# A graph layer's second block per pair as three f32r products, with the powers, the shift and the vector engine's order rearranged

## The chip, the cores and the metric

The kernel runs on one core of a Trainium2 chip. Its time is the device time of one execution in microseconds (us). The core has five engines that run their own instruction streams and meet at semaphores: TensorE (PE; its weight loads are listed as PEld), VectorE (DVE), ScalarE (ACT), GpSimd (POOL) and SyncE (SP), which here only issues DMAs.

## The reference

```python
h = concatenate([x[row], x[col]], axis=-1)          # 25,000 edges, 50,000 nodes, D = 256
msgs = silu(h @ W1.T + b1) @ W2.T + b2
agg = segment_sum(msgs, row) / (cnt + 1e-08)
gi, gh = agg @ w_ih.T + b_ih, x @ w_hh.T + b_hh
r, z = sigmoid(i_r + h_r), sigmoid(i_z + h_z)
n = tanh(i_n + r * h_n)
x_new = (1.0 - z) * n + z * x
gnn = gamma * (x_new - mean) / sqrt(var + 1e-05) + beta
out = layernorm(x + gnn)
```

## The kernel before, in words

There are two stages. The edge stage (0 to about 940 us of the span) makes a message of 768 numbers per edge, already multiplied with `w_ih`, and stores it to DRAM as a high and a low f32r part. The node stage (from about 948 us) takes the 50,000 nodes as 392 blocks of 128, two blocks (h = 0 and 1) to a pair, 196 pairs. One pair is one turn of every engine. `node_turns` writes the order of each engine by hand: a list of (part, lag), where in the step for pair q the engine does `part` for pair q + lag. The first 12 steps are written out, the middle is a loop whose body holds four steps (QU = 4, the number of buffers of most tiles), the last ones are written out again. Every wait is on a semaphore counter `S[...]` that its producer raises once a pair.

For one pair: POOL gathers the messages of both blocks (`gather_rows`, tile `mg`, an indirect DMA each, after `copy_rows` has put four row numbers into `rows_now` for every second pair). DVE makes one-hot matrices (`one_hot`, tile `oh`), PE adds the messages to nodes (`segment_sum`, eight f32r products), ACT scales the sums by the counts (`mean_scale`), PE adds x times `whh` in fp32 and the bias (`node_products`, lines mm L938), ACT takes the sigmoids (`gates`, tile `rz`). Then DVE: `gated_h` (rhn), `n_input` (npre); ACT: `tanh` (nt); DVE: `subtract_n` (diff), `z_diff` (zd), `x_new` (xn), `stats1` (st), `aggregate1` (ag), every second turn `var_eps1` (ve from ag); POOL: `inv_std1` (a power -0.5 of the four variances of two pairs, tile rs1, L420) and `add_beta` (xb = x + beta, L413); DVE: `scale_gamma` (tg), `residual` (uu, with its sum by accumulator), `minus_mean` (nm); ACT: `squares` (with accumulator); DVE: `var_eps2` (ve from sq); POOL: `inv_std2` (two variances, tile rs2, L428); DVE: `shift` (nmr); ACT: `last_norm` (yy); SP stores yy.

DVE's order in a step, and POOL's:

```python
node_turns(dve, ((gated_h, -1), (n_input, -1), (var_eps2, -5), (residual, -4), (one_hot, 2), (minus_mean, -4),
                 (subtract_n, -1), (z_diff, -1), (x_new, -1), (scale_gamma, -3), (stats1, -1), (shift, -5),
                 (aggregate1, -1), (var_eps1, -1)), first=-2, last=5)
node_turns(pool, ((gather_rows, 4), (inv_std1, -2), (inv_std2, -5), (add_beta, -2)), first=-4, last=5)
node_turns(pe, ((products0, 0), (segment_sum, 1), (products1, 0)), first=-1, last=0)
```

`segment_sum` of pair q + 1 waits for `n_input` of pair q - 1, since two sets of PSUM banks alternate.

Of the kernel before, what the change touches and what calls it, by code (L numbers as in the profile page):

```python
# [63 lines left out]
def gnn_layer(nc, x, xt, src, dst, w1t, b1, w2, b2, wiht, whht, bih, bhh, gamma, beta, consts, out):  # L64
# [4 lines left out]
    with ctx:  # L69
# [6 lines left out]
        def sems(name, n):  # L76
# [19 lines left out]
        whh = sb("whh", [P, KC, G3])  # L96
        bias_hn = sb("bias_hn", [P, D], f32r)
# [50 lines left out]
        tg = sb("tg", [P, 2, 2 * D])  # L148
        st1, ag1 = sb("st1", [P, QU, 2, 6]), sb("ag1", [P, QU, 2, 2])
# [11 lines left out]
        idx_ready, w1_hi, w1_ready = sem("idx_ready"), sem("w1_hi"), sem("w1_ready")  # L161
        b2_ready, wc_mm, wc_hi, wc_lo = sem("b2_ready"), sem("wc_mm"), sem("wc_hi"), sem("wc_lo")
# [22 lines left out]
                 " n_s1 n_a1 n_v1 n_r1 n_tg n_u n_nm2 n_sq2 n_v2 n_r2 n_nmr n_y").split()  # L185
# [77 lines left out]
        def _(sp):  # L263
# [63 lines left out]
            def load_x(q, u):  # L327
                need(sp, S["n_mm"], q - QU + 1)
                sp.dma_start(xts[:, u, :], xt[bass.ds(q * P, P), :]).then_inc(got_xt[u], 16)
# [12 lines left out]
            node_turns(sp, ((store_y, -7), (load_counts, 3), (load_x, 3), (load_rows, 2)), first=-3, last=7)  # L342
# [10 lines left out]
        def _(pool):  # L353
# [35 lines left out]
            def node_stage(summed):  # L389
                def copy_rows(q, u):  # L390
                    need(pool, S["n_oh"], q - QU + 2)
                    nc.gpsimd.tensor_copy(rows_now[:, 2 * u:2 * u + 4], slot_row[:, bass.ds(2 * q, 4)])\
                        .then_inc(idx_now, 1)
                    pool.wait_ge(idx_now, 2 * E_TURNS + duo(q, u))

                def gather_rows(q, u):
                    if u % 2 == 0 and not summed:
                        copy_rows(q, u)
                    for h in range(2):
# [5 lines left out]
                        else:  # L405
                            gather(to, rows_now[:, 2 * u + h:2 * u + h + 1], messages, got_m[2 * u + h], last_row)

# [44 lines left out]
        def _(act):  # L452
# [681 lines left out]
```

## Time and profile before

| | |
|---|---|
| median of three runs | 2369.15 us (2367.12 to 2369.52) |
| the profiled execution's own time | 2368.18 us |
| its span, first to last instruction | 2366.2 us |
| busy over the span: PE, DVE, ACT, POOL | 96%, 84%, 63%, 61% |
| mean granted TensorE clock | 0.991 of full |
| 1000 to 2300 us | 184 turns of 7.07 us |

A busy share says how long an engine had an instruction in it, not that it set the pace. PE's is over all matmuls, which overlap each other, so it is read by the distance from one start to the next. For DVE too, instructions overlap a little: the next one can start before the last one's end, and the distance of starts is what an instruction costs.

### The profile page before, as it was taken

To read this page: it belongs to the slowest core of one execution; us is meant where nothing else is said; L and a number is where in the kernel's file an instruction comes from. 1 tells how busy PE (TensorE), PEld (TensorE's weight loads), DVE (VectorE), ACT (ScalarE), POOL (GpSimd) and SP (SyncE) were. 2 spreads that over 40 slices of the span, in tenths; PEclk is the share of its full clock that TensorE was granted. 3 is DMA by queue.
4 is the path that set the end of the run, shared out by engine and by line. 5 is a ranking of instruction groups with operands and counts; after the bars stand their busy time and mean duration, and the time that the engine had idled before them with its cause. 6 is when DMAs were issued, how large, how long until landed. Compare 5 with 4: busy or idle time off the path is not lost.

```text
span 2366.2 us, 46571 instructions
## 1 busy us (share of the span) xinstructions
PE 2278.3 (96%) x10226; PEld 1620.5 (68%) x10226; DVE 1993.6 (84%) x6129; ACT 1500.4 (63%) x2959; POOL 1437.9 (61%) x1479
## 2 busy tenths in 40 slices
PE   6999999999999998899999999999999999999995
PEld 4888888888888886566666666666666666666663
DVE  6777777777777776599999999999999999999998
ACT  3444444444444444477777777777777777777776
POOL 5444444444444441577777777777777777777774
PEclk9999999999999999899999999999999999999998
DMA  4666666666666665666766666666666666666663
GB/s 150 232 231 230 230 231 231 231 228 230 230 229 228 230 232 201 209 222 227 227 227 226 224 229 223 225 222 222 215 223 225 225 223 220 227 219 225 224 217 112
DMA packets 192885, 521.09 MB, mean 220 GB/s; under 512 B 51393, under 2 KB 53977, under 8 KB 192857
## 3 DMA queue, kind: packets, MB, share of 16 engines
q1 hardware_dynamic: 116752, 313.91, 37.1%
q0 software_dynamic: 75264, 206.47, 27.1%
q10 hardware_dynamic: 840, 0.40, 0.1%
q8 instruction: 9, 0.15, 0.0%
q14 instruction: 20, 0.16, 0.0%
HBM read 468.80 MB, written 206.73 MB: 285 GB/s over the span
## 4 chain that ended last, share of the span: by engine, by line
PE 39%; DVE 24%; POOL 16%; issue 16%; DVEq 2%; POOLq 1%; DMA 1%; ACT 0%; SPq 0%; ACTq 0%
PE banks L938 35%; POOL rs L420 6%; POOL mg L347 5%; PE banks L950 4%; DVE zd L869 3%; DVE xn L875 3%; DVE st L916 3%; POOL rs L428 3%; DVE rhn L852 3%; DVE diff L864 3%; DVE tg L880 2%; POOL xb L413 2%; DVE uu L891 2%; DVE ag L922 2%; DVE oh L843 2%
## 5 line engine op out<-in xcount | busy, mean ns | idle before, releaser
L938 PE MATMUL banks<-whh,xts 128*128 128x512 f32 (+1 forms) x3136 | 1089.5, 485 | 0.0
L938 PEld LDWEIGHTS banks<-whh,xts 128*128 128x128 f32 x3136 | 552.2, 190 | 312.5 <-issue 281.8
L347 POOL DMA_INDIRECT mg<-messages,rows_now x392 | 467.9, 1194 | 171.2 <-issue 80.3
L347 POOL DMA_INDIRECT xsrc<-in_x,src_now x196 | 187.1, 954 | 419.3 <-PE banks L950 412.0
L413 POOL TENSOR_TENSOR xb<-xs,betab 128x512 f32<-128x512 f32 x196 | 250.6, 1279 | 198.5 <-DVE ag L922 198.5
L938 PE MATMUL banks<-mg,oh 128*128 128x512 f32 (+1 forms) x1568 | 323.6, 348 | 35.6 <-DVE npre L858 17.6
L480 ACT ACTIVATE msg<-banks 128x512 fp32r<-128x512 f32 (+1 forms) x392 | 192.6, 491 | 244.3 <-PE banks L938 217.1
L542 ACT ACTIVATE banks<-banks,rcount 128x768 f32<-128x768 f32 x392 | 326.7, 871 | 32.2 <-PE banks L938 22.5
L938 PEld LDWEIGHTS banks<-mg,oh 128*128 128x128 f32 x1568 | 253.8, 189 | 126.8 <-issue 75.0
L645 DVE TENSOR_TENSOR msg<-banks,msg 128x512 fp32r<-128x512 f32 (+1 forms) x392 | 200.0, 552 | 152.2 <-ACT msg L480 152.2
L554 ACT ACTIVATE yy<-uu,nmr,rs 128x256 f32<-128x256 f32 x392 | 214.0, 593 | 169.1 <-DVE nmr L911 169.1
L938 PE MATMUL banks<-bias_hn,ones 128*128 128x256 f32 x392 | 266.9, 681 | 0.0
L938 PE MATMUL banks<-wsh,silh 128*128 128x512 f32 (+1 forms) x784 | 264.1, 337 | 2.8 <-DVE msg L645 2.8
L938 PE MATMUL banks<-wsl,silh 128*128 128x512 f32 (+1 forms) x784 | 263.8, 337 | 0.0
L938 PE MATMUL banks<-wsh,sill 128*128 128x512 f32 (+1 forms) x784 | 263.2, 336 | 0.0
L530 ACT ACTIVATE rz<-banks 128x512 f32<-128x512 f32 x392 | 229.0, 584 | 4.8 <-PE banks L938 4.8
L347 POOL DMA_INDIRECT xdst<-in_x,dst_now x196 | 186.5, 951 | 65.1 <-issue 64.8
L548 ACT ACTIVATE nt<-npre 128x512 f32<-128x512 f32 x196 | 123.9, 632 | 155.3 <-DVE npre L858 155.3
L461 ACT ACTIVATE eh<-banks 128x512 fp32r<-128x512 f32 x196 | 117.4, 599 | 164.7 <-PE banks L950 154.5
L564 ACT ACTIVATE yy<-uu,nm 128x256 f32<-128x256 f32 x392 | 194.7, 503 | 2.5 <-DVE nm L900 2.5
L891 DVE SCALAR_TENSOR_TENSOR uu<-tg,rs,xb 128x256 f32<-128x256 f32 x392 | 173.7, 481 | 0.0
L880 DVE SCALAR_TENSOR_TENSOR tg<-xn,ag,gammab 128x256 f32<-128x256 f32 x392 | 171.2, 478 | 0.0
(128 smaller groups left out, 4151.6 us busy)
## 6 DMA issues: line engine op xcount, KB each, us to landing
messages<-msg SPq DMA_DIRECT2D x196, 772.0 KB, 3.3
xts<-in_xt SPq DMA_DIRECT2D x196, 256.0 KB, 6.7
xs<-in_x SPq DMA_DIRECT2D x196, 256.0 KB, 3.6
out_y<-yy SPq DMA_DIRECT2D x196, 256.0 KB, 3.5
mg<-messages,rows_now POOLq DMA_INDIRECT x392, 7.5
xsrc<-in_x,src_now POOLq DMA_INDIRECT x196, 3.5
xdst<-in_x,dst_now POOLq DMA_INDIRECT x196, 2.9
oh<-counts SPq DMA_DIRECT2D x196, 2.0 KB
```

What stands on the lines that cost most here:

```text
L347: nc.gpsimd.indirect_dma_start(out=dst_tile, out_offset=None, in_=rows, in_offset=bass.IndirectOffsetOnAxis(ap=table, axis=0), bounds_chec ...
L413: nc.gpsimd.tensor_tensor(out=xb[:, u, :], in0=xs[:, u, :], in1=betab[:, :], op=ALU.add)\
L420: nc.gpsimd.tensor_tensor(out=rs1[:, u - 1:u + 1, :].rearrange("p q h -> p (q h)"), in0=ve1[:, u - 1:u + 1, :].rearrange("p q h -> p (q h) ...
L480: nc.scalar.activation(msg[:, u % EU, n0:n1], p_g[:, part, 0:n1 - n0], ACT.Copy).then_inc(e_gh[part], 1)
L530: nc.scalar.activation(rz[:, u % 2, h, :], pn[u % 2][:, h, 0, :], ACT.Sigmoid).then_inc(S[f"n_rz{h}"], 1)
L542: nc.scalar.activation(sums_now, sums_now, ACT.Copy, scale=rcount[:, bass.ds(q * 2 + h, 1)])\
L554: last = nc.scalar.activation(yy[:, u, h * D:(h + 1) * D], uu[:, u, h * D:(h + 1) * D], ACT.Identity, bias=nmr[:, u, h:h + 1], scale=rs2[: ...
L564: last = nc.scalar.activation(yy[:, u, h * D:(h + 1) * D], uu[:, u, h * D:(h + 1) * D], ACT.Square, bias=nm2[:, u, h:h + 1], accum_out=sq2 ...
L645: nc.vector.tensor_tensor(msg[:, u % EU, HALF + n0:HALF + n1], p_g[:, part, 0:n1 - n0], msg[:, u % EU, n0:n1].bitcast(f32), ALU.subtract). ...
L880: last = nc.vector.scalar_tensor_tensor(out=tg[:, u % 2, h * D:(h + 1) * D], in0=xn[:, u, h * D:(h + 1) * D], scalar=ag1[:, u, h, 0:1], in ...
L891: last = nc.vector.scalar_tensor_tensor(out=uu[:, u, h * D:(h + 1) * D], in0=tg[:, u % 2, h * D:(h + 1) * D], scalar=rs1[:, u, h:h + 1], i ...
L938: return nc.tensor.matmul(out_, lhsT, rhs, start=start, stop=stop, skip_group_check=skip)
```

## The change

The second block of each pair (h = 1) no longer multiplies x in fp32: ACT copies the block's x to f32r (`x_hi`, tile xh), POOL subtracts that from x (`x_lo`, tile xl), and PE does three f32r products (high by high, high by low, low by high) with f32r halves of the weights, which are made once in the edge stage by an ACT copy and a DVE subtraction, while ACT waits for the latter. `inv_std2` takes the powers of two pairs at once, `shift` and `last_norm` come later (lag -7 for -5 and -6), `squares` writes its unused main output into xn and no longer into yy, `copy_rows` goes ahead by a step, and the orders of POOL, ACT and DVE change.

```diff
+        wxh, wxl = sb("wxh", [P, KC, G3], f32r), sb("wxl", [P, KC, G3], f32r)
+        xh, xl = sb("xh", [P, QU, D], f32r), sb("xl", [P, QU, D], f32r)
...
             def load_x(q, u):
+                need(sp, S["n_xl"], q - QU + 1)
                 need(sp, S["n_mm"], q - QU + 1)
...
-            node_turns(sp, ((store_y, -7), (load_counts, 3), (load_x, 3), (load_rows, 2)), first=-3, last=7)
+            node_turns(sp, ((store_y, -8), (load_counts, 3), (load_x, 3), (load_rows, 2)), first=-4, last=8)
...
+                def x_lo(q, u):
+                    if not isinstance(q, int) or q >= 5:
+                        pool.wait_ge(S["n_tg"], q - 3)
+                    pool.wait_ge(S["n_xh"], q + 1)
+                    need(pool, S["n_mm"], q - QU + 1)
+                    nc.gpsimd.tensor_tensor(out=xl[:, u, :], in0=xts[:, u, D:2 * D], in1=xh[:, u, :].bitcast(f32),
+                                            op=ALU.subtract).then_inc(S["n_xl"], 1)
...
                 def inv_std2(q, u):
-                    pool.wait_ge(S["n_v2"], q + 1)
-                    need(pool, S["n_y"], q - QU + 1)
-                    nc.gpsimd.tensor_tensor(out=rs2[:, u, :], in0=ve2[:, u, :], in1=halves[:, 0:2], op=ALU.pow)\
-                        .then_inc(S["n_r2"], 1)
-
-                node_turns(pool, ((gather_rows, 4), (inv_std1, -2), (inv_std2, -5), (add_beta, -2)), first=-4, last=5)
+                    if u % 2 == 1:
+                        pool.wait_ge(S["n_v2"], q + 1)
+                        need(pool, S["n_y"], q - QU + 1)
+                        nc.gpsimd.tensor_tensor(
+                            out=rs2[:, u - 1:u + 1, :].rearrange("p q h -> p (q h)"),
+                            in0=ve2[:, u - 1:u + 1, :].rearrange("p q h -> p (q h)"),
+                            in1=halves[:, :], op=ALU.pow).then_inc(S["n_r2"], 1)
+
+                node_turns(pool, ((inv_std1, -2), (inv_std2, -5), (x_lo, 1), (add_beta, -2), (gather_rows, 4), (copy_rows, 5)), first=-5, last=5)
...
+            nc.scalar.activation(wxh[:, :, :], whh[:, :, :], ACT.Copy).then_inc(wx_hi, 1)
+            act.wait_ge(wx_lo, 1)
             act.wait_ge(rb_mm, 1)
...
+            def x_hi(q, u):
+                act.wait_ge(got_xt[u], 16 * (nth(q, u) + 1))
+                need(act, S["n_mm"], q - QU + 1)
+                nc.scalar.activation(xh[:, u, :], xts[:, u, D:2 * D], ACT.Copy).then_inc(S["n_xh"], 1)
...
-            node_turns(act, ((last_norm, -6), (tanh, -1), (gates0, 0), (mean_scale, 1), (squares, -4), (gates1, 0)), first=-1, last=7)
+            node_turns(act, ((tanh, -1), (gates0, 0), (mean_scale, 1), (x_hi, 2), (gates1, 0), (last_norm, -7), (squares, -4)), first=-2, last=7)
...
+            dve.wait_ge(wx_hi, 1)
+            nc.vector.tensor_tensor(wxl[:, :, :], whh[:, :, :], wxh[:, :, :].bitcast(f32), ALU.subtract).then_inc(wx_lo, 1)
...
             def x_new(q, u):
                 dve.wait_ge(S["n_zd"], q + 1)
+                need(dve, S["n_sq2"], q - QU + 1)
...
             def shift(q, u):
-                dve.wait_ge(S["n_r2"], q + 1)
+                dve.wait_ge(S["n_r2"], duo(q, u))
...
-            node_turns(dve, ((gated_h, -1), (n_input, -1), (var_eps2, -5), (residual, -4), (one_hot, 2), (minus_mean, -4),
-                             (subtract_n, -1), (z_diff, -1), (x_new, -1), (scale_gamma, -3), (stats1, -1), (shift, -5),
-                             (aggregate1, -1), (var_eps1, -1)), first=-2, last=5)
+            node_turns(dve, ((gated_h, -1), (n_input, -1), (shift, -7), (var_eps2, -5), (var_eps1, -2), (residual, -4), (minus_mean, -4),
+                             (subtract_n, -1), (z_diff, -1), (x_new, -1), (one_hot, 2), (scale_gamma, -3), (stats1, -1),
+                             (aggregate1, -1)), first=-2, last=7)
...
+                        if h == 0:
+                            last = mm(to, xts[:, u, c * P:(c + 1) * P], whh[:, c, n0:n1], False, c == KC - 1, True)
+                        else:
+                            hi, lo = (t[:, u, c * P:(c + 1) * P] for t in (xh, xl))
+                            mm(to, hi, wxh[:, c, n0:n1], False, False, True)
+                            mm(to, hi, wxl[:, c, n0:n1], False, False, True)
+                            last = mm(to, lo, wxh[:, c, n0:n1], False, c == KC - 1, True)
```

## Rows read from the trace of the kernel before

**Rows 1.** Loop, 1000 to 2300 us: busy PE, PEld, DVE, ACT, POOL; clock, DMA

```profile
1000.00:2300.00 1300.00, 1280.73 (x4786) 812.22 (x4785) 1230.80 (x3772) 987.40 (x2026) 970.73 (x920) 1.00 0.68 223
```

**Rows 2.** Waits, same stretch: total us, times, longest

```profile
DVE nmr L911 <- POOL rs L428: 17.3, 90, 1.1
PE banks L938 <- DVE npre L858: 17.2, 47, 1.0
DVE rhn L852 <- issue: 15.7, 44, 0.4
```

**Rows 3.** Timeline of DVE: start us, us busy, what, [idle before]

```profile
1679.50 0.25 DVE L922 BATCH_NORM_AGGREGATE ag<-st 128x2 f32<-128x6 f32 x2
1679.67 0.69 DVE L852 TENSOR_TENSOR rhn<-rz,banks 128x512 f32<-128x512 f32 x1
...
1680.99 0.16 DVE L905 TENSOR_SCALAR ve<-sq 128x2 f32<-128x2 f32 x1
...
1685.31 0.74 DVE L916 BATCH_NORM_STATS2 st<-xn 128x6 f32<-128x256 f32 x2
1685.97 0.14 DVE L911 TENSOR_TENSOR nmr<-nm,rs 128x2 f32<-128x2 f32 x1
1686.20 0.25 DVE L922 BATCH_NORM_AGGREGATE ag<-st 128x2 f32<-128x6 f32 x2
1686.60 0.69 DVE L852 TENSOR_TENSOR rhn<-rz,banks 128x512 f32<-128x512 f32 x1
...
1692.24 0.75 DVE L916 BATCH_NORM_STATS2 st<-xn 128x6 f32<-128x256 f32 x2
...
1693.29 0.25 DVE L922 BATCH_NORM_AGGREGATE ag<-st 128x2 f32<-128x6 f32 x2
1693.89 0.69 DVE L852 TENSOR_TENSOR rhn<-rz,banks 128x512 f32<-128x512 f32 x1 [0.36 <-issue]
...
1700.58 0.25 DVE L922 BATCH_NORM_AGGREGATE ag<-st 128x2 f32<-128x6 f32 x2
...
1701.07 0.69 DVE L852 TENSOR_TENSOR rhn<-rz,banks 128x512 f32<-128x512 f32 x1
```

**Rows 4.** Timeline of DVE near the end of the kernel

```profile
2352.02 0.08 DVE L891 DVE_READ_ACCUMULATOR uu<-tg,rs,xb 128x1 f32 x1
2352.13 0.17 DVE L900 TENSOR_SCALAR nm<-usum 128x2 f32<-128x2 f32 x1
2352.21 0.87 DVE L880 SCALAR_TENSOR_TENSOR tg<-xn,ag,gammab 128x256 f32<-128x256 f32 x2
2353.00 1.22 DVE L911 TENSOR_TENSOR nmr<-nm,rs 128x2 f32<-128x2 f32 x1
```

**Rows 5.** Timeline of POOL near the end of the kernel

```profile
2352.87 1.33 POOL L413 TENSOR_TENSOR xb<-xs,betab 128x512 f32<-128x512 f32 x1
```

**Rows 6.** Timeline of POOL in the loop

```profile
1686.67 1.28 POOL L413 TENSOR_TENSOR xb<-xs,betab 128x512 f32<-128x512 f32 x1 [1.08 <-DVE ag L922]
1688.10 1.31 POOL L347 DMA_INDIRECT mg<-messages,rows_now  x1 [0.15 <-issue]
...
1690.97 1.47 POOL L420 TENSOR_TENSOR rs<-ve,halves 128x4 f32<-128x4 f32 x1
```

**Rows 7.** Timeline of PE in the loop

```profile
1681.22 1.64 PE L938 MATMUL banks<-mg,oh 128*128 128x512 f32 x8
1682.69 1.88 PE L938 MATMUL banks<-whh,xts 128*128 128x512 f32 x4
1684.01 0.68 PE L938 MATMUL banks<-bias_hn,ones 128*128 128x256 f32 x1
...
1686.70 0.68 PE L938 MATMUL banks<-bias_hn,ones 128*128 128x256 f32 x1
```

**Rows 8.** The gathers into mg in the loop, from issue to landing

```profile
DMA to landing us min/median/max: 4.8/7.5/9.2
```

**Rows 9.** Timeline of ACT at the weights' preparation

```profile
34.81 0.60 ACT L499 ACTIVATE bias_c<-banks 128x512 f32<-128x512 f32 x1 [1.71 <-PE banks L938]
```

**Rows 10.** Waits of DVE, 965 to 1003 us, the first turns

```profile
DVE rhn L852 <- PE banks L938: 6.1, 4, 2.8
```

More of the change, by code:

```diff
@@ L161, in gnn_layer @@
         idx_ready, w1_hi, w1_ready = sem("idx_ready"), sem("w1_hi"), sem("w1_ready")
+        wx_hi, wx_lo = sem("wx_hi"), sem("wx_lo")
         b2_ready, wc_mm, wc_hi, wc_lo = sem("b2_ready"), sem("wc_mm"), sem("wc_hi"), sem("wc_lo")
@@ L184, in gnn_layer @@
         names = ("n_oh n_sg0 n_sg1 n_sc0 n_sc1 n_g0 n_g1 n_mm n_rz0 n_rz1 n_rhn n_npre n_tanh n_diff n_xb n_zd n_xn"
-                 " n_s1 n_a1 n_v1 n_r1 n_tg n_u n_nm2 n_sq2 n_v2 n_r2 n_nmr n_y").split()
+                 " n_xh n_xl n_s1 n_a1 n_v1 n_r1 n_tg n_u n_nm2 n_sq2 n_v2 n_r2 n_nmr n_y").split()
         S = {n: sem(n) for n in names}
@@ L390, in copy_rows @@
                 def copy_rows(q, u):
[L391 to L394, printed above, removed]
+                    if u % 2 == 0 and not summed:
+                        need(pool, S["n_oh"], q - QU + 2)
+                        nc.gpsimd.tensor_copy(rows_now[:, 2 * u:2 * u + 4], slot_row[:, bass.ds(2 * q, 4)])\
+                            .then_inc(idx_now, 1)
                 def gather_rows(q, u):
                     if u % 2 == 0 and not summed:
-                        copy_rows(q, u)
+                        pool.wait_ge(idx_now, 2 * E_TURNS + duo(q, u))
                     for h in range(2):
@@ L560, in squares @@
                 need(act, S["n_v2"], q - QU + 1)
-                need(act, n_stored[u], 16 * nth(q, u))
                 for h in range(2):
-                    last = nc.scalar.activation(yy[:, u, h * D:(h + 1) * D], uu[:, u, h * D:(h + 1) * D], ACT.Square,
+                    last = nc.scalar.activation(xn[:, u, h * D:(h + 1) * D], uu[:, u, h * D:(h + 1) * D], ACT.Square,
                                                 bias=nm2[:, u, h:h + 1], accum_out=sq2[:, u, h:h + 1])
@@ L903, in var_eps2 @@
                 dve.wait_ge(S["n_sq2"], q + 1)
-                need(dve, S["n_r2"], q - QU + 1)
                 nc.vector.tensor_scalar(ve2[:, u, :], sq2[:, u, :], 1.0 / D, EPS_LN, ALU.mult, ALU.add)\
@@ L1079, in node_products, with with_x @@
             def node_products(q, u, h):
-                pe.wait_ge(got_xt[u], 16 * (nth(q, u) + 1))
+                if h == 0:
+                    pe.wait_ge(got_xt[u], 16 * (nth(q, u) + 1))
+                else:
+                    pe.wait_ge(S["n_xl"], q + 1)
                 pe.wait_ge(S[f"n_sc{h}"], q + 1)
                 o = pn[u % 2]
-                for c in range(KC):
-                    last = mm(o[:, h, 0, :], xts[:, u, (2 * h + c) * P:(2 * h + c + 1) * P], whh[:, c, 0:2 * D],
-                              False, c == KC - 1, True)
-                last.then_inc(S[f"n_g{h}"], 1)
+                def with_x(to, n0, n1):
+                    for c in range(KC):
+                        if h == 0:
+                            last = mm(to, xts[:, u, c * P:(c + 1) * P], whh[:, c, n0:n1], False, c == KC - 1, True)
+                        else:
+                            hi, lo = (t[:, u, c * P:(c + 1) * P] for t in (xh, xl))
+                            mm(to, hi, wxh[:, c, n0:n1], False, False, True)
+                            mm(to, hi, wxl[:, c, n0:n1], False, False, True)
+                            last = mm(to, lo, wxh[:, c, n0:n1], False, c == KC - 1, True)
+                    return last
+                with_x(o[:, h, 0, :], 0, 2 * D).then_inc(S[f"n_g{h}"], 1)
                 mm(o[:, h, 1, D:2 * D], ones[:, :], bias_hn[:, :], False, False, True)
-                for c in range(KC):
-                    last = mm(o[:, h, 1, D:2 * D], xts[:, u, (2 * h + c) * P:(2 * h + c + 1) * P], whh[:, c, 2 * D:G3],
-                              False, c == KC - 1, True)
-                return last
+                return with_x(o[:, h, 1, D:2 * D], 2 * D, G3)
             def products0(q, u):
```

## The prediction

> **What bounds the kernel now.** The page first suggests TensorE, which is busy for 96% of the span. I then asked for the node stage alone, since almost the whole change lies there: in 1300 us of its loop PE is busy for 1280.7 us and DVE for 1230.8 [rows 1]; 184 turns fit, so a turn is 7.07 us. Two engines near their full time call for a third view, the waits. PE waits for DVE's npre 47 times, about once in every four turns (17.2 us in all), and no wait of DVE for PE is in the list; DVE's own waits are for POOL's power rs before nmr (17.3 us) and an "issue" idle time of 0.36 us once per body of the loop, at its branch [rows 2]. So DVE leads and PE follows. The PE timeline agrees: the sums' eight f32r products take from 1681.22 to 1682.69, 1.47 us, and a fp32 half 2.69 us from one bias product to the next (1684.01 to 1686.70) [rows 7], so PE needs 1.47 + 2 x 2.69 = 6.85 us a turn and has some 0.2 us left. DVE needs 7.07 less what it waits. In the first turns, where DVE lacks the later parts, it is the other way round: DVE waits for PE four times [rows 10].
>
> The question is then what the change does to the distances between DVE's starts. I read those from one turn to the next.
>
> **The change part by part, DVE first; all per turn.**
>
> *The wait for rs2 goes.* From the first st to the first ag it is 0.89 us in the turn without the wait (1685.31 to 1686.20) and 1.05 in the next (1692.24 to 1693.29) [rows 3]. The longer form comes in half the turns, 90 waits in 184 [rows 2]. Hence 0.16 / 2: -0.08. In the new order shift takes a power made two turns earlier, so this should go entirely; at worst (POOL still late) nothing is gained.
>
> *var_eps1 moves* from behind ag, which it waits for, to the middle of small instructions. Before, ag to rhn is 0.17 us without it (1679.50 to 1679.67) and 0.40 and 0.49 with it (1686.20 to 1686.60, 1700.58 to 1701.07) [rows 3]. So 0.23 or 0.32 more in half the turns, 0.14 a turn. In its new place a small instruction costs its issue slot, 0.07 to 0.08 (nm to what follows it, 2352.13 to 2352.21 [rows 4]; its own 0.17 mostly overlaps the next), in half the turns 0.04. Net -0.10; bounds -0.14 and -0.07.
>
> *nmr moves* out of a place where it was free: ag waits for st anyway, and 0.23 us lie between nmr and ag (1685.97 to 1686.20) [rows 3]. Without nmr that gap stays, as ag follows st's end. Behind npre nmr costs its slot: +0.07, at most its own 0.16.
>
> *minus_mean loses its cover.* one_hot stood between uu and nm and moves behind xn. At the end of the kernel, where no one_hot is left, the order uu, nm is already there: nm starts 0.11 us after the accumulator read (2352.02 to 2352.13) [rows 4], whereas in the loop one_hot starts with that read. one_hot costs the same in either place. +0.11; the lower bound is nothing, the upper one 0.2, if diff's own wait for a landing comes late behind nm as well.
>
> *nmr and xb collide.* At the end of the kernel nmr, an operation on two columns that takes 0.14 in the loop [rows 3], takes 1.22 us, from 2353.00 to 2354.22 [rows 4], and POOL's xb runs from 2352.87 to 2354.20 [rows 5]. It was held up until xb was nearly done. In the loop the first candidate today is ve, 1.32 us behind rhn (1679.67 to 1680.99) [rows 3], and xb starts behind ag and takes 1.28 [rows 6], so it is just over in time. In the new order rhn is never held back by ve, while xb still waits for ag: it starts some 0.07 (1686.67 against 1686.60) to 0.2 us behind rhn, later in relation to it by what ve1 used to take. nmr at 1.32 then can wait between nothing and 0.13 us. I take +0.05, the middle rounded down, because ve is never held in the loop today. The Trainium skill, in SBUF — State Buffer, section Who interferes with whom, says that a DVE instruction with two SBUF inputs and a GpSimd instruction that reads SBUF exclude each other, and that whichever is issued first blocks the other. Rows 4 and 5 agree; by its rule every lateness of xb past that point goes to DVE in full, which speaks against taking ve1 out ahead of rhn.
>
> Sum for DVE: -0.08 - 0.10 + 0.07 + 0.11 + 0.05 = +0.05 us a turn. x_new's extra wait (squares a turn earlier) and gated_h's waits stay covered, see ACT and PE.
>
> *PE.* The second half takes twelve f32r products for eight fp32 instructions. Eight f32r ones of the same two widths take 1.47 [rows 7], so twelve 2.2, with the bias product's 0.1 about 2.3 for 2.69: 0.4 us less. PE falls to some 6.45 and just waits longer for npre: nothing on the path. If this cover were gone, x_lo or x_hi late, PE has 0.6 us to absorb it. Only the first turns gain: three of the four waits there (the first one, 2.8 us, is the filling) [rows 10] shrink by 0.4: -1.2 us once.
>
> *ACT* is busy for 987 / 184 = 5.4 us a turn [rows 1]; the copy of 256 columns adds about 0.4 to 0.6. 5.9 of 7.1: hidden. x_hi stands in front of gates1, whose result DVE wants at rhn, over 1.5 us later. tanh now comes first, and DVE wants it at diff: the path npre, nmr, ve, uu, nm to diff is about 1.7 us by the distances above, and tanh of 512 columns needs 0.6 to 0.7. squares comes last in ACT's step and ends before the next tanh; its queue holds nothing that DVE waits for before x_new.
>
> *POOL.* xb to the first gather 1.43, two gathers 2.87 to the power, the power 1.46 [rows 6], half a copy 0.1, and x_lo. x_lo has half of xb's columns: 0.64 if all of xb's 1.28 scales, 1.28 if nothing does; as fixed parts of POOL instructions are small (the copy of four columns) I take 0.73. Together 6.6, and up to 0.2 for the sequencer: 6.6 to 6.8 of 7.1. The second power of each second pair vanishes (it is now one of four columns every second turn, in the turn without inv_std1). So POOL keeps the pace, with 0.3 to 0.5 us to spare. x_lo waits for tg, and add_beta and the gathers are queued behind it; as add_beta waits for the later ag anyway, that wait costs nothing. The gathers come a turn later than before: the second starts some 3 us into a turn and its one_hot reads it 4.9 us into the next one, so it has 8.9 to 9 us, against 7.5 in the median and 9.2 at most [rows 8]. A few turns may wait 0.1: under 1 us in all. With one_hot in its old place, 2.2 us into the turn, it would have had 6.3 and lost.
>
> *SP.* load_x waits for x_lo too, which is a turn older; load_rows still waits for xb at the turn's end and is the last of its step. xts is wanted a turn earlier, by x_hi; it is issued three pairs ahead. Nothing.
>
> *Once.* In the edge stage ACT copies 1536 columns: 0.60 us for 512 [rows 9], so at most 1.8, and 1.5 with a fixed part of 0.15. Then it waits for DVE's subtraction, by the 0.69 us of a 512-column one and the columns' share about 1.8. Before, ACT waited 1.71 us there [rows 9]; 3.3 - 1.7 = +1.6 us, and PE waits behind bias_c. At the end the last power has four columns instead of two and comes in the same chain: +0.5.
>
> **Total.** 184 turns x 0.05 = 9.2. The 12 turns before the loop's start have no wait for rs2, so the other four terms hold, +0.13 for the eight that DVE paces: 1.0. Then -1.2 + 1.6 + 0.5. Sum +11.1 us on the profiled execution's 2368.2: 2379.3. The median of the runs is 1 us above that execution, so 2380.
>
> **The rivals.**
> - *A wait behind its producer is free* (faster). If nm behind uu costs nothing, the turn is 0.05 - 0.11 = -0.06: -11 + 1 = -10, so 2359. For it: only one place of the trace has this order. Against it: that place shows 0.11, and DVE's chain is otherwise gapless. It decides from a cost of nm, nmr and the collision together under 0.17 us. The Trainium skill, in VectorE: DVE Perf Modes, section The DRAIN you can't avoid, says that a semaphore between DVE instructions costs nothing extra. By that rule this rival would be the case; the 0.11 in rows 4 is against it. 0.23, taken with the milder forms in which nmr's slot is free too (2346).
> - *TensorE paces part of the turns after all* (faster). If the 0.36 us at rhn once in four turns were PE and not the branch, 0.09 a turn would go: 0.05 - 0.09 = -0.04, 2362. For it PE's 98% in rows 1; against it the row's "issue" and PE's waits for DVE. 0.07.
> - *The terms cancel* within 0.2%: 0.15.
> - *POOL becomes late* (slower by more). If x_lo takes 1.28 or a gather is late, POOL needs 7.2 to 7.4 us, xb comes late, and DVE's nmr is held by as much: +0.2 a turn, 39 us and more, 2410 to 2430. For it: the spare time is only 0.3 to 0.5 us. 0.14.
> - *My forecast*, slower by 0.2 to 1.3%: 0.41.
>
> **How the numbers follow.** A measurement of this kernel can tell about 0.2% (5 us) from no change. Faster 0.30 (the first two), same 0.15, slower 0.55. The likeliest case's own range is 2374 to 2400; the bounds of its terms added up give -0.08 - 0.14 + 0.07 + 0 + 0 = -0.15 and, the wait gone, -0.08 - 0.07 + 0.16 + 0.2 + 0.13 = +0.34, or 2341 to 2437. For 8 in 10 I leave out the outermost parts: 2348 to 2412.
>
> **What would show it right or wrong.** In the new trace: no wait of DVE nmr for POOL; nm 0.11 behind the accumulator read; nmr near 0.15 to 0.2 us long and not 1 us; PE waiting for npre in every turn, by 0.5 us and more; DVE's busy share of the loop up, from 94.7%; x_lo near 0.73, within st. Wrong would be: nm following at once, a turn under 7.0, DVE waiting for PE, mg or POOL, or nmr long.

## The result: 2421 us, 2.2% slower, and the profile after

The changed kernel takes 2421.18 us (median of 4 runs, 2419.53 to 2421.72), the kernel before beside it 2369.28. The ratio is 1.022, with a 95% interval of 1.0202 to 1.0238. The profiled execution's span is 2419.3 us, before it was 2366.2. I had forecast 2380 with a range up to 2412: the direction is right, the size is not. Of the runs further down, one execution each of d3 and d4 took over twice the time of the others and is left out of their medians.

First the loop's busy time from 1000 to 2300 us (PE, PEld, DVE, ACT, POOL, then clock and DMA), to be held against [rows 1]:

```profile
1000.00:2300.00 1300.00, 1164.26 (x5336) 840.62 (x5335) 1221.31 (x3646) 1002.10 (x2130) 1026.72 (x978) 1.00 0.66 216
```

PE is busy for 116 us less, and everything takes longer all the same: fewer turns fit, and DVE starts 3646 instructions for 3772. DVE's busy share is 93.9% for 94.7%; it fell, where the forecast's list of signs had it rise, since the added time lies between instructions. The waits of the same stretch (total us, times, longest) against [rows 2]:

```profile
PE banks L964 <- DVE npre L883: 135.7, 178, 2.2
POOL xl L419 <- DVE tg L906: 124.0, 175, 1.8
POOL xb L427 <- DVE ag L948: 60.7, 175, 0.5
DVE ag L948 <- DVE st L942: 27.1, 178, 0.2
DVE rhn L877 <- issue: 17.7, 42, 0.4
DVE oh L868 <- DMA mg<-messages,rows_now: 2.6, 6, 0.8
```

PE waits for npre in every turn now, 0.76 us each time; POOL waits for DVE twice a turn; DVE's wait of nmr for the power is gone. What is left to DVE is waiting for itself (ag behind st), the loop's branch and six waits for a gather. So DVE sets the turn. The DVE timeline over one turn and the top of the next, shortened (start, busy time, what it does, idle time before), against [rows 3, 4]:

```profile
1711.70 0.69 DVE L877 TENSOR_TENSOR rhn<-rz,banks 128x512 f32<-128x512 f32 x1
1712.42 0.69 DVE L883 TENSOR_TENSOR npre<-rhn,banks 128x512 f32<-128x512 f32 x1
1713.02 0.15 DVE L937 TENSOR_TENSOR nmr<-nm,rs 128x2 f32<-128x2 f32 x1
1713.09 0.16 DVE L931 TENSOR_SCALAR ve<-sq 128x2 f32<-128x2 f32 x1
...
1713.97 0.08 DVE L917 DVE_READ_ACCUMULATOR uu<-tg,rs,xb 128x1 f32 x1
1714.09 0.45 DVE L926 TENSOR_SCALAR nm<-usum 128x2 f32<-128x2 f32 x1
1714.17 0.69 DVE L889 TENSOR_TENSOR diff<-xs,nt 128x512 f32<-128x512 f32 x1
1714.89 0.71 DVE L894 TENSOR_TENSOR zd<-rz,diff 128x512 f32<-128x512 f32 x1
...
1717.58 0.74 DVE L942 BATCH_NORM_STATS2 st<-xn 128x6 f32<-128x256 f32 x2
1718.47 0.25 DVE L948 BATCH_NORM_AGGREGATE ag<-st 128x2 f32<-128x6 f32 x2 [0.15 <-DVE st L942]
1718.64 0.69 DVE L877 TENSOR_TENSOR rhn<-rz,banks 128x512 f32<-128x512 f32 x1
1719.36 0.69 DVE L883 TENSOR_TENSOR npre<-rhn,banks 128x512 f32<-128x512 f32 x1
1719.96 0.33 DVE L937 TENSOR_TENSOR nmr<-nm,rs 128x2 f32<-128x2 f32 x1
1720.22 0.15 DVE L931 TENSOR_SCALAR ve<-sq 128x2 f32<-128x2 f32 x1
```

And POOL beside it:

```profile
1711.86 1.27 POOL L427 TENSOR_TENSOR xb<-xs,betab 128x512 f32<-128x512 f32 x1 [0.20 <-DVE ag L948]
...
1714.88 1.00 POOL L352 DMA_INDIRECT mg<-messages,rows_now  x1 [0.30 <-issue]
...
1717.74 0.73 POOL L419 TENSOR_TENSOR xl<-xts,xh 128x256 fp32r<-128x256 f32 x1 [0.22 <-DVE tg L906]
1719.01 1.27 POOL L427 TENSOR_TENSOR xb<-xs,betab 128x512 f32<-128x512 f32 x1 [0.55 <-DVE ag L948]
```

The reader is to see three things. nm starts 0.12 us behind the accumulator read (1713.97 to 1714.09). ag starts 0.89 us behind the first st (1717.58 to 1718.47) in every turn. And nmr is 0.15 us long in one turn and 0.33 in the next: in the first xb starts 0.16 us behind rhn (1711.70 to 1711.86), in the second 0.37 (1718.64 to 1719.01), ends at 1720.28, and ve starts at 1720.22.

A single turn misleads, since the loop's body holds four turns that differ. I therefore worked out from the timelines of both kernels the mean distance from each DVE start to the next, over the node turns 12 to 179, apart for the four places in the body. These are the distances that changed (us a turn; forecast beside them):

```
                                           before  after  difference  forecast
st to ag (the wait for rs2, nmr)           0.647   0.559    -0.09      -0.08
first ag to rhn (var_eps1 gone from it)    0.414   0.329    -0.08      -0.14
var_eps1's slot in its new place             -     0.035    +0.03      +0.04
nmr's slot                                   -     0.070    +0.07      +0.07
nmr held up, beyond its slot                 -     0.076    +0.08      +0.05
accumulator read to nm                       -     0.113    +0.11      +0.11
ve (from sq) to what follows it            0.069   0.106    +0.04        0
nm to diff                                 0.070   0.100    +0.03        0
diff to zd to xn                           1.460   1.490    +0.03        0
xn (or uu) to oh, oh, next                 1.125   1.156    +0.03        0
whole turn                                 7.074   7.326    +0.25      +0.05
```

Outside the loop's steady part: DVE's first npre is at 976.51 us for 969.12 before. From npre of turn 12 to that of turn 184 it is 1259.9 us for 1216.7, +43.2. The rest adds 2.5, which makes the span's 53.1.

### The profile page after: what moved, and what is told of

Read it like the earlier page. It is cut to its first block, busy times and chain, and to the rows that moved or that the text cites. A ratio compares the mean times of both kernels' runs of the same rounds, so it can differ in the third digit from the quotient of the medians.

```text
span 2419.3 us, 49124 instructions
## 1 busy us (share of the span) xinstructions
PE 2200.4 (91%) x11010; PEld 1684.5 (70%) x11010; DVE 2029.1 (84%) x6130; ACT 1558.6 (64%) x3156; POOL 1539.6 (64%) x1577
## 4 chain that ended last, share of the span: by engine, by line
DVE 40%; PE 38%; issue 12%; DMA 5%; DVEq 3%; POOL 1%; ACT 0%; SPq 0%; POOLq 0%; ACTq 0%
PE banks L964 34%; DVE tg L906 6%; DVE uu L917 5%; DMA mg<-messages,rows_now 5%; DVE zd L894 5%; DVE st L942 5%; DVE diff L889 5%; DVE rhn L877 5%; DVE oh L868 4%; PE banks L976 4%; DVE ag L948 2%; DVE nmr L937 1%; DVEq L868 1%; DVE ve L931 1%; POOL mg L352 1%
## 5 line engine op out<-in xcount | busy, mean ns | idle before, releaser
L964 PE MATMUL banks<-whh,xts 128*128 128x512 f32 (+1 forms) x1568 | 561.1, 485 | 0.0
L352 POOL DMA_INDIRECT mg<-messages,rows_now x392 | 443.2, 1131 | 96.1 <-issue 89.4
L964 PEld LDWEIGHTS banks<-whh,xts 128*128 128x128 f32 x1568 | 269.2, 189 | 151.5 <-issue 141.1
L964 PE MATMUL banks<-wxh,xl 128*128 128x512 f32 (+1 forms) x784 | 264.6, 338 | 0.0
L964 PE MATMUL banks<-wxl,xh 128*128 128x512 f32 (+1 forms) x784 | 264.3, 337 | 0.0
L964 PE MATMUL banks<-wxh,xh 128*128 128x512 f32 (+1 forms) x784 | 264.1, 337 | 0.0
L419 POOL TENSOR_TENSOR xl<-xts,xh 128x256 fp32r<-128x256 f32 x196 | 143.3, 731 | 138.2 <-DVE tg L906 136.2
```

Of the source, the lines that this page charges most:

```text
L352: nc.gpsimd.indirect_dma_start(out=dst_tile, out_offset=None, in_=rows, in_offset=bass.IndirectOffsetOnAxis(ap=table, axis=0), bounds_chec ...
L419: nc.gpsimd.tensor_tensor(out=xl[:, u, :], in0=xts[:, u, D:2 * D], in1=xh[:, u, :].bitcast(f32), op=ALU.subtract).then_inc(S["n_xl"], 1)
L964: return nc.tensor.matmul(out_, lhsT, rhs, start=start, stop=stop, skip_group_check=skip)
```

## The experiments

A ratio is always to the kernel before, run beside it. A turn is the mean over the turns 12 to 179 of the profiled execution.

**e1: nmr back behind st.** One part of the change undone.

```
- (gated_h, -1), (n_input, -1), (shift, -7), ... (stats1, -1), (aggregate1, -1)
+ (gated_h, -1), (n_input, -1), ... (stats1, -1), (shift, -7), (aggregate1, -1)
```

> The changed kernel with shift put back between stats1 and aggregate1 (its lag stays -7, so the power is still two turns old). Theory (VectorE's own order sets the turn; nmr there lies in a gap in which ag waits for st anyway): nmr's slot of 0.07 us goes, but ve from sq now is the first small operation behind npre and meets xb as nmr did, so only 0.07 a turn is saved, 196 x 0.07 = 14 us, 2407. Rival a (only nmr, with its two SBUF inputs, is held up by xb, and ve is not): 0.15 a turn, 29 us, 2392. Rival b (GpSimd or TensorE sets the turn): 2421.

Measured: 2538.27 us, ratio 1.0719 (1.0701 to 1.0737), a turn of 7.91 us. A plain miss. Its waits in the loop:

```profile
ACT yy L578 <- DVE nmr L937: 385.9, 162, 2.6
...
DVE ve L931 <- ACT xn L587: 90.2, 161, 0.8
```

ScalarE's new order has yy, which needs nmr, ahead of the squares, whose sums ve needs. With nmr late, ACT stands 2.3 us for it, the squares come late, and ve waits. nmr can't simply be put back: ScalarE's new order needs it early. This run says nothing on nmr's price.

**e2: minus_mean behind subtract_n**, so that nm no longer follows the read that it waits for.

```
- (minus_mean, -4), (subtract_n, -1), (z_diff, -1)
+ (subtract_n, -1), (minus_mean, -4), (z_diff, -1)
```

> The changed kernel with minus_mean moved behind subtract_n, so that diff lies between uu and nm, and nm lies between diff and z_diff, which waits for diff anyway. Theory (nm behind its producer costs 0.11, and its own slot can hide in the gap of 0.12 between diff and zd): 0.11 + 0.08 + up to 0.03 of the register work = about 0.2 us a turn, 196 x 0.2 = 39 us, 2382. Rival (a wait behind its producer is free, the turn is long for another reason): 2421, nothing.

Measured: 2383.33 us, ratio 1.0061 (1.0044 to 1.0078), turn 7.142. As expected (2382). On its DVE timeline diff follows the read at once, and nm lies in the gap that zd needs anyway:

```profile
1695.83 0.69 DVE L889 TENSOR_TENSOR diff<-xs,nt 128x512 f32<-128x512 f32 x1
1696.44 0.16 DVE L926 TENSOR_SCALAR nm<-usum 128x2 f32<-128x2 f32 x1
1696.55 0.69 DVE L894 TENSOR_TENSOR zd<-rz,diff 128x512 f32<-128x512 f32 x1
```

diff to zd is 0.72 us with nm in it, and by the distances it is 0.72 in the kernel before without. One edit gives back 38 of the 52 us: more than the 0.11, because nm's own slot (0.07 to 0.10) goes with it, which the kernel before had paid too.

**e3 and e4: the f32r products and the copies.** e3 takes both blocks in fp32 and keeps the copies and their waits; e4 drops x_hi and x_lo as well.

```
-                        if h == 0:
+                        if h < 2:
                             last = mm(to, xts[...], whh[:, c, n0:n1], False, c == KC - 1, True)
```

> The changed kernel with the fp32 products for the second block again, xh and xl still made and still waited for. Theory (TensorE has 0.8 us a turn to spare in the changed kernel and still 0.4 with fp32): 2421, within 4 us, a little above it because of the first turns, which TensorE paces. Rival (TensorE's relief is worth something in the loop, too): 196 x 0.1 to 0.4 us slower, 2440 or more.

> As the one with fp32 products for both blocks, but without the copies xh (ScalarE) and xl (GpSimd). Theory: in the changed kernel xb starts 0.29 and 0.37 us behind rhn in two of four turns and holds up nmr by 0.1 and 0.18; if xl in front of it is what makes it late, nmr is free again, and 0.07 us a turn goes, 14 us, 2407. Rival a (GpSimd's lateness comes from its register work alone): 2421. Rival b (GpSimd's or ScalarE's added work is the whole cost of the change): 2369 or less.

Measured: e3 2421.89 us (1.0229, 1.0212 to 1.0246), e4 2421.64 (1.0221, 1.0204 to 1.0238), turns 7.324 and 7.337. PE's 0.4 us a turn is worth nothing, and so is POOL's 0.73. My theory of e4 (x_lo makes xb late) fell. The number is that of its rival a, but not for that rival's reason: xb waits for ag in every turn (322.6 us in 178 waits), so it is late because of DVE's ag and not of POOL's own work.

**f1: xb earlier.**

```
-                    pool.wait_ge(S["n_a1"], ...)
+                    pool.wait_ge(S["n_s1"], ...)
```

> The changed kernel with one wait altered: add_beta (xb) waits for stats1 of the pair two on (n_s1) instead of aggregate1 (n_a1), so xb can start about 0.3 us earlier and be over before nmr's turn. Theory (xb, which starts 0.16 to 0.37 us behind rhn in three of four turns, holds nmr up; npre to ve is 0.146 us for a slot of 0.07): nmr falls to 0.15 us in every turn type, the turn loses 0.076 us, 184 turns 14 us: about 2407 us, ratio 1.016. Rival (the time between npre and ve is DVE's own and has nothing to do with xb): 2421, ratio 1.022. A second rival: xb earlier meets ag, and ag is held by it instead: 2421 as well, but with ag to rhn longer.

Measured: 2405.72 us, ratio 1.0156 (1.014 to 1.0172), turn 7.243. As expected (2407). In the third turn of the body, where nmr had been held longest, xb now starts 0.03 us ahead of rhn at 1680.07. nmr is 0.15 us long and free, but from ve to the next start it is 0.12 us for a slot of 0.07:

```profile
1680.04 1.28 POOL L427 TENSOR_TENSOR xb<-xs,betab 128x512 f32<-128x512 f32 x1
```

```profile
1681.40 0.15 DVE L937 TENSOR_TENSOR nmr<-nm,rs 128x2 f32<-128x2 f32 x1
1681.47 0.21 DVE L931 TENSOR_SCALAR ve<-sq 128x2 f32<-128x2 f32 x1
1681.59 0.16 DVE L954 TENSOR_SCALAR ve<-ag 128x4 f32<-128x4 f32 x1
```

On average nmr to ve falls from 0.146 to 0.103; the rest of the gain lies at zd, xn and the second oh, which come sooner by 0.05 together. The hold-up of nmr by xb is shown. xb isn't what holds ve at 1681.47, since it ends at 1681.32; POOL's next instruction, a gather, starts at 1681.48.

**c3: both repairs.**

> The changed kernel with both repairs that were tried apart: minus_mean behind subtract_n, and add_beta waiting for stats1. Theory (the two costs are separate terms of DVE's sum): 2421.2 less 37.9 (minus_mean alone) less 15.5 (xb alone) = 2368 us, ratio 0.999 to 1.001, where the kernel before is. Rival (another wait, a gather or GpSimd's power, takes the place of what is gained, since the turn is 0.28 us shorter): 2375 to 2384.

Measured: 2361.64 us, ratio 0.9973 (0.9963 to 0.9982), turn 7.010. The terms add, and 6 us more: e2 still waited for gathers ahead of oh (11.0 us in 25 waits), and with xb, and so the gathers, earlier that is gone. The changed kernel with two small instructions better placed is a quarter of a per cent faster than before.

**g1: one_hot alone moved, in the kernel before.**

```
- (residual, -4), (one_hot, 2), (minus_mean, -4), ... (x_new, -1), (scale_gamma, -3)
+ (residual, -4), (minus_mean, -4), ... (x_new, -1), (one_hot, 2), (scale_gamma, -3)
```

> The kernel before with one thing changed: one_hot moves from between residual and minus_mean to behind x_new, so that minus_mean follows the accumulator read that it waits for. Theory (a small operation behind the producer it waits for costs about 0.11 us, and the register work behind it another 0.03): the turn grows by 0.11 to 0.14 us, 184 turns 20 to 26 us: 2389 to 2395 us, ratio 1.009 to 1.011. Rival (a wait behind its producer is free, and the cost seen in the changed kernel belongs to the whole set of edits): 2369, ratio 1.000.

Measured: 2383.03 us, ratio 1.0061 (1.0047 to 1.0075), turn 7.144: half of what was expected. The DVE timeline has the cost as forecast:

```profile
1696.31 0.08 DVE L891 DVE_READ_ACCUMULATOR uu<-tg,rs,xb 128x1 f32 x1
1696.42 0.45 DVE L900 TENSOR_SCALAR nm<-usum 128x2 f32<-128x2 f32 x1
```

Read to nm is 0.116 on average and nm to diff 0.098 for 0.070, +0.14 in all. But st to ag falls from 0.647 to 0.574: with the longer turn the power is in time, and DVE's nmr waits for POOL 3 times in the loop for 90. So here the wait was the slack of a chain: DVE had it because it was quick elsewhere. The -0.08 that I booked for shift's new place comes in g1 with the longer turn alone. Not every longer turn does it (h1 below still has 88 such waits), and d1 below loses the wait with a shorter one: there POOL needs 5.96 us from xb's start to the end of the second of two powers, for 6.47 in the kernel before.

**h1: the f32r products alone, in the kernel before.**

> The kernel before with the f32r products of the second block alone: x_hi in ScalarE's order behind mean_scale, x_lo in GpSimd's behind inv_std2 with its wait for scale_gamma three turns back, the second block three f32r products; powers for one pair, the old order on DVE, shift five turns late, squares into yy and copy_rows inside gather_rows as before. Theory (DVE sets the turn; x_lo's 0.73 us lies in GpSimd's order ahead of xb and the gathers and behind the powers that nmr waits for): TensorE's relief is unused and the powers, xb and the gathers come later; +0.0 to +0.3 us a turn, 2370 to 2430 us, ratio 1.00 to 1.026. Rival (TensorE's relief of 0.4 us a turn pays by itself): under 2362, ratio under 0.997.

Measured: 2399.71 us, ratio 1.0127 (1.0111 to 1.0142), turn 7.223. PE's relief isn't used, and st to ag grows from 0.65 to 0.91 us. The powers aren't later (88 waits of nmr and 18.1 us, for 90 and 17.3). What grows is nmr itself, on average 0.68 us in the turns of two powers and 0.34 in the others, for 0.14 to 0.16, while xl runs beside it. DVE, then POOL:

```profile
1686.25 0.68 DVE L934 TENSOR_TENSOR nmr<-nm,rs 128x2 f32<-128x2 f32 x1 [0.18 <-POOL rs L442]
1686.85 0.23 DVE L945 BATCH_NORM_AGGREGATE ag<-st 128x2 f32<-128x6 f32 x2
```

```profile
1686.19 0.72 POOL L419 TENSOR_TENSOR xl<-xts,xh 128x256 fp32r<-128x256 f32 x1
```

This is the collision of nmr and xb once more, with xl in xb's place: +0.26 us a turn. The changed kernel, where xl runs beside st, has 0.56 from st to ag.

**b1, c1, d1: every small instruction in a gap.** b1 is the changed kernel with DVE's order as below, copy_rows ahead of x_lo, the gathers five pairs ahead in POOL's order instead of four, and xb as in f1. c1 is b1 with fp32 for both blocks and no x_hi and x_lo. d1 is the kernel before with this order on DVE (var_eps1 a turn later, lag -2 for -1) and nothing else of the change.

```
+ (gated_h, -1), (n_input, -1), (residual, -4), (subtract_n, -1), (var_eps2, -5), (var_eps1, -2),
+ (z_diff, -1), (minus_mean, -4), (x_new, -1), (one_hot, 2), (scale_gamma, -3), (stats1, -1),
+ (shift, -5), (aggregate1, -1)          # shift: -6 in b1 and c1
```

> The changed kernel with another order: DVE gated_h, n_input, residual, subtract_n, var_eps2, var_eps1, z_diff, minus_mean, x_new, one_hot, scale_gamma, stats1, shift (six turns late), aggregate1, so that every small instruction stands in the gap between two large ones that depend on each other (st and ag, diff and zd, zd and xn); add_beta waits for stats1; POOL's order inv_std1, inv_std2, copy_rows, x_lo, add_beta, gather_rows. Theory (DVE's sum sets the turn, a small instruction in such a gap costs nothing, behind its producer 0.11 us): nmr, ve, nm leave the chain, the turn falls from 7.33 to 6.7 to 6.9 us, that is 2300 to 2340 us, ratio 0.97 to 0.99. Rival a (TensorE or the gathers, which come later here, pace the kernel below 7.07 us a turn): 2369 or more. Rival b (the gaps cost the same wherever the small ones stand): 2421.

> The order with the small instructions in the gaps (2328.5 us with f32r products for the second block), with both blocks' x in fp32 and neither x_hi nor x_lo; the other copies in the edge stage stay. Theory (TensorE needs 1.47 + 2 x 2.69 = 6.85 us a turn then, and the turn with f32r is 6.845 by DVE's sum, with one turn in four 0.4 us longer and the others shorter, in which TensorE now has no time to catch up): 6.86 to 6.90 us a turn, 2331 to 2338 us, ratio 0.984 to 0.987. Rival (GpSimd without x_lo is what pays): under 2328, ratio under 0.983. Second rival (the f32r products carry the whole gain): 2360 or more.

> The kernel before (fp32 x, one power per pair, shift five turns late, nothing of the change's other parts) with DVE's order alone altered so that each small instruction stands in a gap: gated_h, n_input, residual, subtract_n, var_eps2, var_eps1 (two turns late), z_diff, minus_mean, x_new, one_hot, scale_gamma, stats1, shift, aggregate1. Theory (the order is the whole gain, GpSimd's power and the gathers only have to be in time): var_eps2's slot 0.07, var_eps1's 0.17 and, if rs2 is in time, the wait's 0.11 leave the chain's 7.07: 6.82 to 6.93 us a turn, 2325 to 2345 us, ratio 0.982 to 0.990. Rival (GpSimd's power comes after the gathers, so nmr waits for it in every turn once the turn is shorter, and the powers for two pairs with the later shift are what makes the short turn possible): 2350 or more.

Measured: b1 2328.53 us, ratio 0.9829 (0.9814 to 0.9844), turn 6.845; c1 2325.25, 0.9819 (0.9805 to 0.9832), 6.823; d1 2323.42, 0.9804 (0.9789 to 0.9819), 6.823. d1's DVE timeline:

```profile
1653.38 0.68 DVE L864 TENSOR_TENSOR diff<-xs,nt 128x512 f32<-128x512 f32 x1
1653.99 0.16 DVE L905 TENSOR_SCALAR ve<-sq 128x2 f32<-128x2 f32 x1
1654.06 0.16 DVE L928 TENSOR_SCALAR ve<-ag 128x4 f32<-128x4 f32 x1
1654.12 0.68 DVE L869 TENSOR_TENSOR zd<-rz,diff 128x512 f32<-128x512 f32 x1
1654.73 0.16 DVE L900 TENSOR_SCALAR nm<-usum 128x2 f32<-128x2 f32 x1
1654.84 0.69 DVE L875 TENSOR_TENSOR xn<-zd,nt 128x512 f32<-128x512 f32 x1
```

diff to zd is 0.74 us with two small instructions in it, against 0.72 with none. The rival of d1 (the power comes too late without the change's other parts) fell: nmr waits for it 3 times, 3.1 us. d1 is 1.6 us below the range that I gave, c1 6 us below its own, where its first rival (POOL without x_lo is what pays) had it; as c1 drops x_hi, x_lo and the f32r products together, what brings it the 3.3 us over b1 isn't separated. d1 has the whole gain with four names moved, while b1 with all of the change's work is no faster. In d1 PE is busy for 1295.8 of the loop's 1300 us and needs, with fp32, as long as DVE; so f32r could pay only with a DVE faster than 6.82.

**c2: DVE's loop body of eight turns** instead of four, on b1.

> The same order with f32r products, and DVE's loop body of eight turns in place of four (the other engines' stays at four). Theory (the branch and the register work at the top of the body and after it cost DVE 0.50 us ahead of rhn, 0.09 behind it and 0.2 ahead of subtract_n, once in a body): half of 0.79 us goes from every four turns, 0.10 us a turn, 18 us: 2310 us, ratio 0.975. Rival (the register work comes with each turn's own waits, only the branch is per body): 2316 to 2322. Rival b (TensorE or GpSimd paces now): 2328.

Measured: 2480.06 us, ratio 1.0477 (1.0461 to 1.0493). A miss by 170 us. Its waits and its DMA queues in the loop:

```profile
DVE rhn L878 <- issue: 112.7, 39, 6.5
DVE diff L890 <- issue: 49.4, 19, 2.8
```

```profile
q14 instruction: 103, 0.84, 0.2%
```

The queue that carries instructions moves 103 packets in the loop's 1300 us, where b1 has 8. DVE stands 5.8 us on average at the top of each body, at most 6.5, and 2.6 once more, at most 2.8. The profile lists 277 DVE instructions in a pass of eight turns and 143 in b1's pass of four. The longer body is loaded again in each pass, the shorter one is not; where between them the limit lies was not tried.

**c4, d2, d3, d4: the edge stage, and where DVE's code stands.** c4 is e4 without the copy and the subtraction of the weights. d2 is c4 with one DVE instruction of one column ahead of the node loop; d3 and d4 are the changed kernel with four and with one of them.

```
+            nc.vector.memset(unused[:, :], 0.0)
             node_turns(dve, ...)
```

> The changed kernel with fp32 x for both blocks, without x_hi and x_lo (2421.6 us measured) and now without the copy and the subtraction of the weights in the edge stage (wxh, wxl) either. Theory (they cost about 3 us once, by the later start of TensorE behind bias_c and what comes of it): 2418.5 us. Rival (the edge stage takes them in later, at another wait): 2421.6.

> The kernel of 2412.3 us (fp32 x, no copies, none in the edge stage either) with one DVE instruction of one column put in right ahead of the node loop, so that the loop's code stands where it stood with 2421.6 us. Theory (the position of DVE's code sets the small gaps: 7.303 us a turn there, 7.336 with one more instruction ahead): the turn goes back to 7.33, 2418 us, with 0.21 us ahead of uu in one turn of four in place of 0.12. Rival (the edge stage alone made the difference): 2412, turn 7.30.

> The changed kernel with four DVE instructions of one column each right ahead of the node loop. Theory (position of the code matters): another distribution of the small gaps, the turn between 7.28 and 7.37, 2413 to 2430 us. Rival (position is nothing): 7.326 and the same gaps, 2421.

> The changed kernel with one DVE instruction of one column right ahead of the node loop. Theory (position of the code matters): the gap of 0.21 us ahead of uu in one turn of four, or that behind nm, moves; the turn between 7.28 and 7.37, 2413 to 2430 us. Rival (position is nothing): 7.326 and the same gaps, 2421.

Measured: c4 2412.27 us, 6 us less than expected; e4 had 2421.64. The first npre is 3.6 us earlier (about 3 expected), but the turn also falls from 7.337 to 7.303, though nothing in the loop's code differs. d2 2417.98, turn 7.332: one instruction ahead brings it back. The larger change is the distance ahead of uu in one turn of four, 0.21 in e4 and d2, 0.12 in c4. The one between the two ag moves as well, 0.14 for 0.10, but c4 has those 0.04 us behind the second ag instead. The DVE timeline of c4:

```profile
1691.03 0.16 DVE L926 TENSOR_SCALAR ve<-sq 128x2 f32<-128x2 f32 x1
1691.15 0.48 DVE L912 SCALAR_TENSOR_TENSOR uu<-tg,rs,xb 128x256 f32<-128x256 f32 x1
```

and of e4:

```profile
1698.94 0.16 DVE L930 TENSOR_SCALAR ve<-sq 128x2 f32<-128x2 f32 x1
1699.16 0.48 DVE L916 SCALAR_TENSOR_TENSOR uu<-tg,rs,xb 128x256 f32<-128x256 f32 x1
```

d3 has 2419.85 us and a turn of 7.320, d4 2425.43 and 7.353: there the extra gap between the two ag is gone, and in d4 another of 0.11 stands ahead of ag in one turn of four. d4's three executions spread from 2420.6 to 2427.1, so its time alone says little. c4 (2408.7 to 2414.7) and d2 (2417.3 to 2419.9) don't overlap. So where DVE's code stands moves gaps of 0.04 to 0.11 us, some 0.03 us a turn or 6 us in all; that the engine fetches its code in pieces is my reading, not shown.

## Why the forecast was too low

*Which engine sets the turn: right.* DVE paces and PE follows. PE waits 0.76 us a turn, e3 shows its relief worth nothing, and the twelve f32r products with the bias product take 2.19 us (1714.73 to 1716.92 on PE's timeline of the changed kernel) for the 2.3 I had.

*The wait for rs2: right in size (-0.09 for -0.08), but shift's new place isn't needed for it.* g1 loses the same wait with shift where it was.

*var_eps1: mis-sized.* I wrote 0.23 or 0.32 for half the turns, net -0.10, and it is -0.05. In the two turns that had it the distance falls by 0.23 and 0.24 us. But the turn at the loop's branch gained 0.14: there ag to rhn was 0.51 with nothing in between and is 0.60, and the two ag are 0.04 further apart. I had counted the branch's time as fixed.

*nmr's slot and the collision with xb: the mechanism was right, the size 0.03 too low.* nmr is held in the turns in which xb starts 0.3 us and more behind rhn (0.175 and 0.257 for 0.07 to 0.08). f1 takes 15.5 us off, and h1 has the same with xl. The Trainium skill, SBUF — State Buffer, section Who interferes with whom, has DVE instructions with two SBUF inputs and GpSimd's reads exclude each other; the trace agrees, with nmr's 0.33 us and ve's start 0.06 ahead of xb's end, and h1's with nmr's 0.68 us beside xl's 0.72.

*minus_mean without cover: the term was right at 0.11 (0.113 measured), and too small for what was at stake.* The rival in which a wait behind its producer is free is refuted twice, by g1 (0.116) and by e2. The Trainium skill, VectorE: DVE Perf Modes, section The DRAIN you can't avoid, has the semaphore cost nothing extra, as measured there in a chain of eight copies. Here nm starts 0.11 us behind the read that it waits for, where oh, which doesn't wait, starts with the read; and zd starts 0.72 us behind the diff that it waits for, where nm in e2 starts 0.61 behind it. The measurement decides against the rule for this chain. Whether the 0.11 us is the semaphore's or the emptying of the engine isn't separated, since every instruction here that needs the one ahead of it also waits for its semaphore.

*The step that failed is the sum.* I added five terms and set the other distances at nothing, one of them in words (one_hot "costs the same in either place"). They are +0.13 us a turn: nm to diff, uu's start behind ve, diff to xn, the two oh, each 0.03 to 0.04 on average and most of it in one or two turns of four.

- The distance ahead of uu moves with the position of the code (c4 and d2, 0.02 us a turn).
- nm to diff is 0.16 in one turn of the body and 0.08 in the others, in g1 too. I had this only in the upper bound of minus_mean's term.
- Of oh's 0.03, about half is the six waits for a gather.
- zd and xn go by POOL's starts. In the fourteen kernels in which xn follows zd directly I took the mean from zd to xn apart for the four places of the body. In 27 of the 56 a POOL instruction starts within 0.03 us of zd, and they have 0.737 to 0.785 us; of the 29 others all but one have 0.725 to 0.728 (e2's fourth turn has 0.746). Above, the gather starts at 1714.88 and zd at 1714.89. The changed kernel has three such places in four, the kernel before one. The coincidence is shown, what POOL's start takes from DVE is not, and no run here moves such a start alone.

With var_eps1 (0.05) and the collision (0.03) the rest makes up the 0.20 by which the turn was missed, 37 of the 42 us. The outer bounds of my terms (+0.34 us a turn, 2437 us) held the measured +0.25; I narrowed them to 2412 for 8 in 10 without a row for it.

*Once: +8.5 us up to turn 12, where I had +1.4.* Three parts make up nearly all of it, 1.5, 1.5 and 5.1 us. The first is the copy and the subtraction of the weights. From the third wsh copy to bias_c ACT needs 4.06 us (32.01 to 36.07) for 2.58 (32.23 to 34.81 [rows 9]), +1.48 for the +1.6 of my forecast; its wait for the subtraction replaces that for PE, as I had it. The kernel before, then the changed one:

```profile
32.23 0.87 ACT L497 ACTIVATE wsh<-banks 128x512 fp32r<-128x512 f32 x2 [1.71 <-PE banks L938]
```

```profile
32.01 0.87 ACT L514 ACTIVATE wsh<-banks 128x512 fp32r<-128x512 f32 x2 [1.71 <-PE banks L964]
32.77 1.49 ACT L515 ACTIVATE wxh<-whh 128x1536 fp32r<-128x1536 f32 x1
36.07 0.60 ACT L518 ACTIVATE bias_c<-banks 128x512 f32<-128x512 f32 x1 [1.82 <-DVE wxl L704]
```

The second I had left out, TensorE's clock. PE stands 2.50 us ahead of 37.04, where it stood 1.01 us before, and from 37.5 to 40.9 us the granted clock is 0.5, the lower level of 1.2 GHz. Busy times and clock of 37 to 41 us, first before, then after:

```profile
37.00:41.00 4.00, 4.00 (x22) 2.73 (x20) 3.69 (x13) 2.01 (x3) 2.84 (x2) 1.00 0.12 33
```

```profile
37.00:41.00 4.00, 3.96 (x14) 3.05 (x14) 2.10 (x8) 0.60 (x1) 0.97 (x1) 0.57 0.00 0
```

Nine of the thirteen kernels with the copies show this stretch of 3.4 us, and they need 19.2 to 19.3 us from bias_c to ACT's first message; the other four with the copies (c3, d3, e3, f1) and the five without them need 17.7 to 17.8. So the lower clock costs 1.5 us, in the profiled execution of the changed kernel too. The edge stage's end scatters besides, by 4 us among kernels with the same edge stage, so that the 3.6 us between c4 and e4 are not the price of the copies alone.

The third was not foreseen. From the last messages' store to POOL's first gather of the node stage it is 11.1 us for 6.0 before. In the eleven kernels here that have x_lo in POOL's body it is 9.1 to 11.1, in the seven without it 5.9 to 6.0. So the time comes with the longer body. In each of the eleven a packet of the instruction queue starts 1.6 to 2.4 us ahead of POOL's first copy of that stage (954.8 and 956.54 in the changed kernel), in the seven none does. That POOL waits there for its code is likely by this; whose code the packet holds the trace doesn't say.

*POOL right, the gathers a little too low.* x_lo takes 0.73 us, the powers are in time, and the gathers cost 2.6 us in 6 waits, where I had under 1. DVE's list of waits shows none for a load by SP.

## What to carry to other kernels

In DVE's chain here a small instruction costs by its place: between independent ones its slot of 0.07 us, behind the producer that it waits for 0.11 us more, between two large instructions that depend on each other nothing. Put the small ones there first; it was worth 2% here with four names moved, while the work taken from PE and POOL in e3 and e4 changed nothing. Nor should a small DVE operation on two SBUF tiles stand where GpSimd works on large ones in SBUF: nmr cost 0.08 us a turn more beside xb and 0.26 beside xl. And before an engine that merely follows is relieved, check that the wait to be removed isn't the slack of a chain that will take it back: g1 lost rs2's wait by becoming slower, and d1 by making POOL's chain shorter.

A forecast by distances has to take every distance of the loop's body, each of its turns apart, and leave room for those that it sets at nothing.

## What the runs showed that I had not expected

- DVE's loop body of 143 instructions runs from what the engine holds, one of 277 is loaded anew in each pass: 5.8 us and 2.6 us of standing per pass, 103 packets of instructions for 8.
- One instruction more ahead of the loop changes the turn by 0.03 us (7.303 to 7.332, c4 and d2).
- An nmr that comes some 5 us later in DVE's turn costs 117 us (e1; 2538.3 for 2421.2), through ScalarE's order and not through DVE's.
- Between the edge stage and the node stage POOL stood 3 to 5 us longer once its body had one more operation.
- A pause of PE of 2.50 us in the edge stage was followed by 3.4 us at the lower clock in nine kernels and not in four.
